# Moving blends, products for the maxima and the next layer's routing to earlier steps of an attention layer

## The reference

```
x = x + L0_attention(layernorm(x), ctx)      # layer 0: 16 heads of 8, 77 keys a batch
x = x + L0_experts(layernorm(x))             # layer 1: the best 4 of 16 experts a row
x = x + L1_attention(layernorm(x), ctx)      # layer 2
x = x + L1_experts(layernorm(x))             # layer 3: the best 1 of 8 experts a row
x = x + L2_local_attention(ctx, layernorm(x))
x = x + L2_mha_and_experts(layernorm(x))
x = x + L3_attention(layernorm(x), ctx)
x = x + L3_gated_experts(layernorm(x))

# attention
q, k, v = split(xn @ Wq.T + bq), split(ctx @ Wk.T + bk), split(ctx @ Wv.T + bv)
s = (q @ k.T * tau + delta) / sqrt(8)
out = softmax(s) @ v @ Wo.T + bo
```

## Time and profile before

| | |
|---|---|
| median of 3 runs | 1052.99 us (1052.76 to 1057.67) |
| profiled execution | 1051.74 us |
| its span | 1049.9 us |
| PE busy | 751.1 us (72%) |
| DVE busy | 621.5 us (59%) |
| ACT busy | 344.6 us (33%) |
| POOL busy | 261.2 us (25%) |

### The profile page before, as it was taken

The page is one execution under the profiler, slowest core; times in us unless marked ns, Lnnn a source line. Parts: engine busy times, 40 slices in busy tenths (PEclk is TensorE's granted clock), DMA queues, the critical chain, the costliest instruction groups (busy, mean ns, idle before and its releaser), DMA issues.

```text
span 1049.9 us, 13386 instructions
## 1 busy us (share of the span) xinstructions
PE 751.1 (72%) x3940; PEld 466.1 (44%) x3940; DVE 621.5 (59%) x1995; ACT 344.6 (33%) x584; POOL 261.2 (25%) x305
## 2 busy tenths in 40 slices
PE   2578772848849657577585745876887678689998
PEld 1123331848838412223373634474654323245554
DVE  6657756326224435666442536789786767666764
ACT  2455420524415234233221112212232365432231
POOL 4050366440242371710323032212111100000000
PEclk9589865869959867767796876898998899789999
DMA  5135021433523340206112010010210111000000
GB/s 162 46 103 209 18 80 62 124 93 109 151 83 87 106 109 11 70 27 215 50 42 83 21 38 1 1 68 4 70 34 13 45 58 33 1 1 11 11 11 10
DMA packets 70784, 64.87 MB, mean 62 GB/s; under 512 B 9076, under 2 KB 62637, under 8 KB 70202
## 3 DMA queue, kind: packets, MB, share of 16 engines
q1 hardware_dynamic: 53178, 47.36, 15.4%
q0 software_dynamic: 5120, 10.50, 3.4%
q10 hardware_dynamic: 12416, 6.16, 2.0%
HBM read 34.94 MB, written 22.54 MB: 55 GB/s over the span
## 4 chain that ended last, share of the span: by engine, by line
PE 46%; DVE 24%; issue 16%; ACT 4%; POOL 3%; SPq 3%; DMA 1%; another core or an unknown queue 1%; DVEq 0%; ACTq 0%; POOLq 0%
PE psum_all L884 5%; PE psum_all L900 5%; DVE s_nmx L1325 3%; PE psum_all L796 3%; PE psum_all L778 3%; PE psum_all L780 3%; PE psum_all L691 3%; PE psum_all L669 3%; PE psum_all L671 2%; PE psum_all L650 2%; DVE s_x_normed L1226 2%; PE psum_all L766 2%; PE psum_all L606 2%; DVE s_h L1463 1%; PE psum_all L744 1%
## 5 line engine op out<-in xcount | busy, mean ns | idle before, releaser
L2493 POOL TENSOR_SCALAR s_vare<-s_mv 128x4 f32<-128x4 f32 x40 | 11.8, 295 | 456.3 <-DVE s_mv L1218 456.2
L1325 DVE TENSOR_REDUCE s_nmx<-psum_all 128x4 f32<-128x308 f32 x192 | 83.3, 473 | 58.8 <-PE psum_all L650 36.1
L2078 ACT ACTIVATE s_hT<-psum_all 77x1024 f32<-77x1024 f32 x96 | 95.8, 1017 | 65.2 <-PE psum_all L671 44.1
L650 PE MATMUL psum_all<-s_ks,s_t 128*128 128x308 bf16 x192 | 61.1, 365 | 52.2 <-DVE s_nmx L1325 27.5
L669 PE MATMUL psum_all<-s_t,s_ks 128*77 128x512 bf16 x192 | 85.2, 444 | 11.4 <-ACT s_hT L2078 8.5
L671 PE MATMUL psum_all<-s_t,s_ks 128*77 128x512 bf16 x192 | 83.7, 436 | 0.0
L1583 DVE COPY s_t<-s_arena 128x256 f32 x94 | 21.6, 292 | 99.4 <-remote 47.4
L2413 POOL DMA_INDIRECT s_w<-routed_y,s_cT x64 | 61.9, 967 | 72.7 <-issue 72.7
L691 PE MATMUL psum_all<-s_hT,s_v 77*32 77x512 f32 x384 | 61.1, 711 | 25.2 <-ACT s_hT L2078 24.1
L900 PE MATMUL psum_all<-s_arena,s_hT 128*128 x376 | 62.8, 303 | 22.0 <-issue 21.6
L2399 POOL DMA_INDIRECT routed_x<-s_x_normed,s_cT x64 | 63.2, 987 | 47.5 <-DVE s_cT L1522 28.7
(11 more groups left out here) (315 smaller groups left out, 1578.6 us busy)
## 6 DMA issues: line engine op xcount, KB each, us to landing
s_t<-q_parts SPq DMA_DIRECT2D x60, 128.0 KB, 2.9
routed_y<-s_hT ACTq DMA_DIRECT2D x22, 256.0 KB
s_ks<-s_att SPq DMA_DIRECT2D x72, 77.0 KB, 2.1
s_arena<-in_w SPq DMA_DIRECT2D x2, 2048.0 KB, 11.9
q_parts<-s_qparts SPq DMA_DIRECT2D x10, 384.0 KB
s_h<-routed_x SPq DMA_DIRECT2D x48, 64.0 KB
s_x_normed<-routed_x SPq DMA_DIRECT2D x46, 64.0 KB
routed_x<-s_w SPq DMA_DIRECT2D x34, 64.0 KB
```

The costliest lines, as they stand in the source:

```text
L650: pe.matmul(o, T1[:, u % QS, g, 128 * i:128 * i + 128], KS1[:, HPG * g:HPG * g + HPG, SK * b:SK * b + SK], start=True, stop=True))
L1325: read(job, dve.tensor_reduce(nmx[:, u % 2, i, HPG * g:HPG * g + HPG], PS[:, k, 0:HPG * SK].rearrange("p (h s) -> p h s", h=HPG), AX.X, AL ...
L2078: read(("S", L, b, p), nc.scalar.activation(Eexp[:, (PAIRS * u + p) % ES, :, :], PS[0:SK, k:k + 2, :], ACT.Exp))
```

## The change

Stages of layer 2 move to other steps, and POOL's list is cut in other places. No instruction is added or dropped. In turn 0, M3 goes from step 5 to 3, MT from 7 to 6, and both blends of batch 2 and its stats stand there together. In turn 1, front and Q go from steps 4 and 5 to 2 and 3, M0 from 7 to 6, and both blends of batch 3, its stats and its norm now stand in this turn. In turn 2, front and Q go from 2 and 3 to 0 and 1, M0 and M1 from 7 to 5 and 6, and layer 3's norms and both fronts stand in this turn. In turn 3, R goes from 2 to 1 and rank from 3 to 2. The output products move one to three steps forward.

```diff
 LATE_PLACES = {
...
-    (2, 2): [((0, 0, 0), "norm", 2, 3), ((2, 0, 2), "front", 2, 3),
...
+    (2, 2): [((0, 0, 0), "front", 2, 3), ((1, 2, 1), "Q", 2, 3), ((5, 5, 0), "M0", 2, 3), ((6, 6, 0), "M1", 2, 3),
...
@@ -2469,9 +2469,8 @@
                 if (which, L, b) == ("in", 2, 2):
                     routed_gather(2, range(0, 16))
-                    routed_gather(3, range(0, 6))
-                if (which, L, b) == ("in", 2, 3):
-                    routed_gather(3, range(6, 16))
+                    routed_gather(3, range(0, 10))
+                if (which, L, b) == ("in", 3, 0):
                     for x in range(4, 8):
                         pool.wait_ge(s_rga[x], 16 * 2 * TOPK)
                     sorted_tables()
@@ -2493,6 +2492,8 @@
                 pool.tensor_scalar(vare[:, n % 2, :], mv[:, n % 2, :, 1], EPS, None, ALU.add).then_inc(s_vare, 1)
                 pool.wait_ge(s_vare, n + 1)
                 pool.tensor_tensor(rstd[:, n % 2, :], vare[:, n % 2, :], mhalf[:, :], ALU.pow).then_inc(s_rstd, 1)
+                if (which, L, b) == ("in", 2, 2):
+                    routed_gather(3, range(10, 16))
                 if which == "in" and LAYERS[L] == ATTN:
```

More of the change, by code:

```diff
@@ L65 @@
 LATE_PLACES = {
[6 rows of a table removed]
-    (2, 2): [((0, 0, 0), "norm", 2, 3), ((2, 0, 2), "front", 2, 3),
-             ((3, 3, 3), "Q", 2, 3), ((7, 7, 6), "M0", 2, 3), ((7, 7, 6), "M1", 2, 3), ((7, 7, 7), "M2", 2, 3),
-             ((7, 7, 7), "M3", 2, 3), ((7, 7, 7), "MT", 2, 3)],
+    (2, 0): [((0, 0, 0), "M0", 2, 1), ((1, 1, 0), "M1", 2, 1), ((2, 2, 0), "M2", 2, 1), ((3, 3, 0), "M3", 2, 1),
+             ((6, 3.1, 6), "MT", 2, 1), ((0, 4.5, 0), "combine0", 1, 2), ((0, 4.6, 0), "combine1", 1, 2),
+             ((0, 4.7, 0), "stats", 2, 2)],
[6 rows of a table added]
 }
 SORTED_PLACES = {
-    2: {("stats", 0): (0, 3.2, 0), ("norm", 0): (0, 3.4, 0), ("front", 0): (5, 0, 5), ("stats", 1): (0, 6.1, 0)},
-    3: {("norm", 1): (0, 0.1, 0), ("front", 1): (1, 0, 1), ("R", 0): (2, 2, 3),
-        ("rank", 0): (3, 0, 0), ("slots", 0): (0, 3, 0), ("stats", 2): (0, 5.2, 0)},
+    2: {("stats", 0): (0, 2.2, 0), ("norm", 0): (0, 3.1, 0), ("stats", 1): (0, 3.2, 0), ("front", 0): (4, 0, 4),
+        ("norm", 1): (0, 5.1, 0), ("front", 1): (6.2, 0, 6.2)},
+    3: {("R", 0): (1, 1, 1), ("rank", 0): (2, 0, 0), ("slots", 0): (0, 2, 0), ("stats", 2): (0, 4.2, 0)},
 }
-EPILOGUE = {0: (3.5, 7, 7), (0, 3): (0.2, 3, 3), 2: (3.5, 5, 6), (2, 1): (0.9, 6, 6), (2, 2): (1.5, 5, 6), (2, 3): (0.5, 5, 5),
+EPILOGUE = {0: (3.5, 7, 7), (0, 3): (0.2, 3, 3), 2: (3.5, 5, 6), (2, 1): (0.9, 4, 4), (2, 2): (0.5, 3, 3), (2, 3): (0.5, 4, 4),
             6: (3.5, 7, 7), 7: (3.5, 8, 8)}
```

## The result

The changed kernel took 1063.32 us (median of 10 runs, 1060.69 to 1069.68), the kernel before 1055.34 (10 runs). The ratio is 1.0073, 95% interval 1.0047 to 1.0099: slower by 0.7%, where I had forecast no change and put 1061 at the top of the range. In a second group of runs it was 1.0106 (1.0069 to 1.0143). My forecast of 1053.0 started from the median of three runs of the kernel before; over ten runs that median is 2.35 us higher. Of the 10.3 us between forecast and time, 2.35 are this base and 8.0 the change.

A forecast was written before the change was run, and what follows sets the result against it. No engine was full (chain PE 46%, DVE 24%, issue 16%), so order and waits in turns 0 to 3 mattered. Terms +3.8 - 1.1 - 1.7 - 1.0 = 0.0 gave 1053.0 us, range 1044 to 1061.

The forecast's parts named there:

- The crawl follows the gathers: Turn 0: DVE and ACT stand nearly idle during POOL's first gather block, going on 3.4 us behind its last gather.
- c: Time the crawl adds in turn 0 through four more gathers: 3.8 us, bounds 0 and 5.0.
- Turns 0 and 1, -1.1: Earlier queries bring batch 2's first maximum 2.3 us sooner, the norm costs 1.1; turn 2 begins 1.1 sooner, plus c.
- My +1.0 for turn 0: Turn 0's new orders: turn 1 begins at 415.6 + c instead of 414.6.
- Turn 2, -1.7: Half of batch 3's maxima products go among scores; MT ends 36.7 us into turn 2 against 38.4.
- the three stops of ACT: Turn 2: new waits before exponentials, at fronts of batch 3 (step 0) and layer 3's batches 0 and 1 (steps 4, 6).
- Turn 3, -1.0: R one step earlier brings rank, slots, scatters and layer 3's product 1.0 us sooner; bounds 3.1 and 0.
- The clock "stays as it is": The granted clock stays at 0.68 to 0.84 in the four turns.
- B: Rival: the crawl does not follow the gathers, c = 0, time 1049.2 us; chance 0.14.
- C: Rival: the crawl also covers turn 1's second gather block, over front and Q, costing 7.9 us: 1060.9; chance 0.18.
- A: Rival: overlap works as drawn, ACT's stops cost nothing, 11.3 us sooner in all: 1041.7; chance 0.19.
- D: Rival: orders change but no wait does, since DMA landings set all; within 1 us of 1053; chance 0.03.

The follow-up runs named there:

- 26/6: Kernel before with only POOL's gathers cut 26 and 6 instead of 22 and 10: 1.0042 of the kernel before with the crawl, 1.0004 and 0.9958 without.
- before_blends: Kernel before with batch 2's second blend and statistics moved from turn 1 to the end of turn 0: 1.0048 of the kernel before, without the crawl.
- act_late: Changed kernel with ScalarE's copies of layer 3's two fronts in turn 2 one exponential later: 1.0032 of the kernel before, with the crawl.
- combo: Changed kernel with gathers 22 and 10, turn 0's M3 and MT at old places, turn 2's two front copies later: 1.0081 with the crawl, 0.9971 without.

## Why the prediction was wrong

- **The crawl follows the gathers**: right, shown by 16, 22 and 26 gathers. The size was off: I put c at 3.8, since I assumed the added time would be used at a quarter of the full pace; it is 5.0 with the old orders (turn 0 of 26/6: 37.3 - 32.3). What I called a pace was work done early in the stretch; in its last part nothing ran.
- **Turns 0 and 1, -1.1**: +0.2 beside the block in the first trace (7.0 - 5.0 - 1.8), and +2.2 to +4.7 in three further traces of the same orders (74.4 to 77.0 us for the two turns, 72.2 for the old orders with the same 26 gathers). My +1.0 for turn 0 was 2.0 or more, which fits the 1.4 to 1.9 us of before_blends. The part I had worked out in detail, the first maximum 2 us sooner behind the crawl, came true (2.1), but the turn did not keep it. This is a second term that I had too low.
- **Turn 2, -1.7**: the step that failed. It measured +5.6, far above my upper bound of 1.1. I had named the three stops of ACT, and then followed the engines to 36.7 without a figure for any of them. They were 16.3 us against 7.7 before, and act_late gave back 5.1 to 5.6 us of the turn by moving two copies behind one exponential each. The bound was wrong in kind: it counted only work added to DVE, no wait added to ACT.
- **Turn 3, -1.0**: +0.4. R stood at 7.15 instead of the forecast 6.4, rank at 13.6 instead of 12.1 (13.2 before), and the slots at 15.8, where the kernel before had 15.2. The exponential behind R stopped ACT as I had said, for 6.03 us (3.60 before).
- **The clock "stays as it is"**: not quite. In turn 2 it was 0.65 and 0.61 in the changed kernel, 0.68 before and in act_late. It was lower where the stops were longer, and 1.8 of the 5.2 us between the changed kernel and act_late are PE's instructions taking longer. So by the profile the clock carries part of the price of the stops; whether it fell because of them was not tested apart.
- **Rivals**: B is wrong with the crawl and right without. C's place was wrong for this kernel, but its mechanism showed in combo with the crawl. A is wrong: even with the two stops cut to half, turn 2 was no shorter than before. D is wrong, since the turns moved by up to 7.0 us.
- **The signs of being wrong** that I gave, turn 2 below 34 us or a crawl that does not move, did not appear: both looked for less time than forecast, none for a turn that grows.

By the profile the sum is +5.0 + 0.2 + 5.6 + 0.4 = 11.2, where I had 0.0. The medians say 8 and 12 in the two groups. Turn 2's part is shown by a run that takes it away, the block's part for the old orders alone; the split of turns 0 and 1 is an account of one trace, not shown.

## What to carry to other kernels

An early place for a stage is a place on every engine that takes part. Before you move one, look at each engine for what is queued behind the waiting instruction, and price that wait as the time until its input can exist. Here it helped to put the consumer's place one item later than the producer's: 5.1 to 5.6 us in a turn of 44. A block of indirect DMAs held up the other engines until it ended in one of two conditions of this program, so its length is worth a term of the sum even where no data depend on it. Where a bound is set for a stage, add the waits, not only the work.

## What was unexpected of the hardware

- The same program has two conditions, 1055 us and 982 us, whole groups of runs in one of them. The same chip met the one in one group and the other in another, so the chip alone does not decide it. With the crawl, PE, DVE and ACT stand in the last part of a long block of indirect DMAs, with single instructions between, and are back at full pace 2 to 4 us behind it (in the old orders DVE 1.9, 3.4 and 3.8 us behind with 16, 22 and 26 gathers). What makes the standstill was not found: for the last long wait before DVE and ACT go on, the profile names nothing that they waited for ("remote", with 16 gathers "issue").
- Turn 3 with the old R took either 29.9 to 30.1 us (three traces; granted clock 0.84) or 32.4 to 33.1 (eight; 0.71); with the early R it took 29.8 to 30.3 in all nine, at 0.73 or 0.78. So the early R gains nothing on the best traces and some 2.7 us on the others, and the profile of the kernel before was one of its good ones.
- What lies behind layer 3's first product took 527 to 541 us in these traces, though no kernel changes it. Most of the difference arises in layers 3 to 5: 292 to 307 us, at a mean granted clock from 0.86 down to 0.80, while the rest took 233 to 235. The medians of 9 to 12 runs have intervals of 0.3 to 0.4% to each side, so an effect of 0.5% is at the edge of what they can show.
